# A four-layer graph network: the spread destination row loaded from ScalarE's queue, the third turn beside the first two, one TensorE wait out, node stores one round earlier

## What is computed

```python
x = _layernorm(x + _L0_gnn_ref(x, node_vec1, edge_attr_3, edge_attr_64, src, dst, ...), axis=-1)
x = _layernorm(x + _L1_gnn_ref(x, node_vec1, edge_attr_16, edge_attr_4, src, dst, ...), axis=-1)
x = _layernorm(x + _L2_gnn_ref(x, node_vec1, edge_attr_4, edge_attr_8, ..., src, dst, 16), axis=-1)
x = _layernorm(x + _L3_gnn_ref(x, node_vec1, src, dst, edge_attr_4, edge_attr_64, ...), axis=-1)
```

```python
amax = jax.lax.stop_gradient(jax.ops.segment_max(a, edge_dst, num_segments=n))
a = jnp.exp(a - amax[edge_dst])
a = a / (jax.ops.segment_sum(a, edge_dst, num_segments=n)[edge_dst] + 1e-12)
ns = jax.ops.segment_sum(vs * a[..., None], edge_dst, num_segments=n).reshape(n, H * H0)
```

```python
m_v3 = w5[:, :, None] * jnp.cross(ev, e1[:, None, :]) * _inv(2)
agg_s = jax.ops.segment_sum(mid_s, edge_dst, num_segments=n) * inv_nn
agg_v = jax.ops.segment_sum(mid_v, edge_dst, num_segments=n) * inv_nn
o_s = agg_s @ lin2_ws * a * _inv(S_MID)
...
pre_s = sc_s + o_s
pre_v = sc_v + o_v
scalars = jax.nn.silu(pre_s[:, :64])
gates = jax.nn.sigmoid(pre_s[:, 64:96])
gated = gates[:, :, None] * pre_v
```

## Time and profile before

| | us |
|---|---|
| median of 3 executions | 8838.66 |
| lowest, highest | 8814.75, 8842.85 |
| the profiled execution | 8821.47 |
| its span | 8819.7 |

### The profile page before, as it was taken

The page is one execution under the profiler, slowest core; times in us unless marked ns, Lnnn a source line. Parts: engine busy times, 40 slices in busy tenths (PEclk is TensorE's granted clock), DMA queues, the critical chain, the costliest instruction groups (busy, mean ns, idle before and its releaser), DMA issues. The chain is left out here.

```text
span 8819.7 us, 169625 instructions
## 1 busy us (share of the span) xinstructions
PE 6072.5 (69%) x36496; PEld 5115.7 (58%) x36496; DVE 6244.2 (71%) x20178; ACT 4194.7 (48%) x10003; POOL 4731.4 (54%) x4424
## 2 busy tenths in 40 slices
PE   3767777776657777777776666777666678884444
PEld 3555555555556666656665655666566567774443
DVE  6967777777658887866565775666688878785666
ACT  2544444443325555544444775444466645553333
POOL 3456666664445555545444554445466544445666
PEclk9977777776559999988888887889788899996666
DMA  6732222224753333334444665444466544443444
GB/s 185 242 119 75 75 76 75 77 71 133 205 168 105 108 110 103 106 92 120 116 117 131 198 196 158 116 116 120 122 178 179 172 120 129 128 122 115 128 128 124
DMA packets 774197, 1137.24 MB, mean 129 GB/s; under 512 B 322032, under 2 KB 410038, under 8 KB 773648
## 3 DMA queue, kind: packets, MB, share of 16 engines
q1 hardware_dynamic: 591952, 831.36, 30.2%
q0 software_dynamic: 182144, 304.74, 15.4%
HBM read 667.03 MB, written 472.87 MB: 129 GB/s over the span
## 5 line engine op out<-in xcount | busy, mean ns | idle before, releaser
L718 POOL DMA_INDIRECT agg<-seg_rows,node_idx x1568 | 1530.1, 976 | 1137.2 <-issue 924.4
L457 POOL DMA_INDIRECT erow<-e_rows,ids x1176 | 1220.0, 1037 | 1282.4 <-issue 1176.6
L397 PE MATMUL banks<-w_all,xt 128*128 128x128 f32 (+1 forms) x2352 | 559.7, 375 | 939.8 <-DVE stats L755 424.4
L397 PEld LDWEIGHTS banks<-w_all,xt 128*128 128x128 f32 x2352 | 439.2, 251 | 1027.9 <-issue 999.5
L767 POOL TENSOR_TENSOR stats<-stats,power 128x4 f32<-128x4 f32 (+1 forms) x392 | 524.8, 1339 | 544.6 <-DVE stats L755 341.9
L655 POOL DMA_INDIRECT row_of_dram<-where x392 | 431.7, 1101 | 559.0 <-DMA where<-place_dram 417.9
L487 PE MATMUL banks<-w_all,mid 128*128 128x128 f32 (+1 forms) x2744 | 457.9, 293 | 395.4 <-ACT hid_p L538 355.0
L400 PE MATMUL banks<-w_all,xt 128*128 128x128 f32 x3528 | 658.5, 339 | 0.0
L487 PEld LDWEIGHTS banks<-w_all,mid 128*128 128x128 f32 (+1 forms) x2744 | 327.7, 146 | 524.0 <-ACT hid_p L538 415.7
L400 PEld LDWEIGHTS banks<-w_all,xt 128*128 128x128 f32 x3528 | 620.9, 254 | 0.0
L544 ACT ACTIVATE radial<-banks 128x768 f32<-128x768 f32 (+1 forms) x294 | 248.6, 846 | 650.1 <-PE banks L497 362.1
(11 more groups left out here) (282 smaller groups left out, 18272.0 us busy)
## 6 DMA issues: line engine op xcount, KB each, us to landing
x_rows<-xo SPq DMA_DIRECT2D x294, 324.0 KB
xin<-x_rows SPq DMA_DIRECT2D x294, 324.0 KB
e_rows<-ets SPq DMA_DIRECT2D x294, 322.0 KB
dst_row<-in_dst_flat SPq DMA_DIRECT2D x294, 256.0 KB
xin<-in_x SPq DMA_DIRECT2D x196, 324.0 KB
seg_rows<-res SPq DMA_DIRECT2D x196, 322.0 KB
seg_rows<-res SPq DMA_DIRECT2D x98, 384.0 KB
seg_rows<-res SPq DMA_DIRECT2D x98, 338.0 KB
```

The source lines that it names most:

```text
L397: pe.matmul(flat[:, to + k * cols:to + (k + 1) * cols], of[:, k * P:(k + 1) * P], W(w_s), start=True, stop=True)
L457: pool.indirect_dma_start(erow[s.quad][:, t, 0:EROW], None, table, bass.IndirectOffsetOnAxis(ids[s.quad][:, t:t + 1], 0),).then_inc(edges_ ...
L718: pool.indirect_dma_start(agg[s.quad][:, t, 0:SUM_COLS[layer]], None, seg_rows[layer], bass.IndirectOffsetOnAxis(node_idx[s.slot][:, t, 0: ...
```

## The change

There are four edits.

- Edge softmax: `row_back` is no longer loaded by SP in `load` but by ScalarE, in a new function `load_row` at the head of ScalarE's list. It waits for the same count of `pre_step` as SP's `load` does and signals a semaphore of its own, which VectorE awaits before the comparison. ScalarE's other functions move from delays 0, 0, 2 to 3, 3, 5; what they wait for is unchanged.
- Edge stage of layer 3 (the lists of layers 1 and 2 come out as before): `turn_part` 2 on TensorE, and its copy on ScalarE, stand directly behind parts 0 and 1 instead of behind `weights`.
- Node stages 1 to 3: SP's stores stand one round earlier (5 and 6 instead of 6 and 7; in layer 3, 5 instead of 6). The title in a few words does not mention this.
- Node stage of layer 3: TensorE's wait for `sum_step` in `back` is left out. In layers 1 and 2 it stays.

```diff
-        soft_in = [signal(f"soft_in_{k}", 48, 2) for k in range(4)]
+        soft_in = [signal(f"soft_in_{k}", 32, 2) for k in range(4)]
+        row_back_in = [signal(f"row_back_in_{k}", 16, 2) for k in range(4)]
...
                     pipeline(pe, chunks, [
-                        (hidden, 0), (lambda s: turn_part(s, 0), 2), (lambda s: turn_part(s, 1), 2), (sums, 4), (weights, 0),
-                        *[(lambda s: turn_part(s, 2), 2)][:parts - 2], (linear, 2)])
+                        (hidden, 0), (lambda s: turn_part(s, 0), 2), (lambda s: turn_part(s, 1), 2),
+                        *[(lambda s: turn_part(s, 2), 2)][:parts - 2], (sums, 4), (weights, 0), (linear, 2)])
...
                     pipeline(act, chunks, [
-                        (hidden, 0), (lambda s: copy_part(s, 0), 2), (lambda s: copy_part(s, 1), 2), (weights, 0),
-                        *[(lambda s: copy_part(s, 2), 2)][:parts - 2], (sums, 4), *[(wrap, 0)][:crossed], (linear, 2)])
+                        (hidden, 0), (lambda s: copy_part(s, 0), 2), (lambda s: copy_part(s, 1), 2),
+                        *[(lambda s: copy_part(s, 2), 2)][:parts - 2], (weights, 0), (sums, 4), *[(wrap, 0)][:crossed], (linear, 2)])
...
-                        pipeline(sp, chunks, [loads, (lambda s: store_nodes(sp, s, x_rows[layer + 1]), 6),
-                                              (lambda s: store_e(sp, s, layer + 1), 7)])
+                        pipeline(sp, chunks, [loads, (lambda s: store_nodes(sp, s, x_rows[layer + 1]), 5),
+                                              (lambda s: store_e(sp, s, layer + 1), 6)])
                     else:
-                        pipeline(sp, chunks, [loads, (store_out, 6)])
+                        pipeline(sp, chunks, [loads, (store_out, 5)])
...
                         pe.wait_ge(xt_sb.sem, xt_sb.after(s.g + 1))
-                        pe.wait_ge(sum_step.sem, sum_step.after((s.g - 1 + with_e) * sum_steps - with_e * (sum_steps - read)))
+                        if with_e:
+                            pe.wait_ge(sum_step.sem, sum_step.after(s.g * sum_steps - (sum_steps - read)))
                         pe.wait_ge(pre_step.sem, pre_step.after((s.g - 1) * pre_steps))
...
-                        sp.dma_start(to_row[s.quad][:].rearrange("p t e -> p (t e)"),
-                                     inp["dst_flat"][0, bass.ds(c * CHUNK, CHUNK)].partition_broadcast(P)).then_inc(edges.sem, 16)
...
+                        dve.wait_ge(row_back_in[s.quad].sem, row_back_in[s.quad].after(s.quarter + 1))
                         dve.wait_ge(cols_in[b].sem, cols_in[b].after(s.quarter + 1))
...
-                    pipeline(act, chunks, [(exponentials, 0), (copy, 0), (sums, 2)])
+                    def load_row(s):
+                        c = chunks - 1 - s.g
+                        precompute(act, pre_step.after((s.g - 3) * 3))
+                        act.wait_ge(ready.sem, 1)
+                        act.wait_ge(pre_step.sem, pre_step.after((s.g - 3) * 3))
+                        act.dma_start(to_row[s.quad][:].rearrange("p t e -> p (t e)"),
+                                      inp["dst_flat"][0, bass.ds(c * CHUNK, CHUNK)].partition_broadcast(P)) \
+                            .then_inc(row_back_in[s.quad].sem, 16)
+
+                    pipeline(act, chunks, [(load_row, 0), (exponentials, 3), (copy, 3), (sums, 5)])
```

More of the change, by code:

```diff
@@ L1681, in edge_softmax @@
                 sig.passed(chunks // 2)
-            for sig, n in (*zip(soft_in, of_quad), *zip(soft_values, of_quad), *zip(cols_in, of_pair), *zip(place_in, of_pair), *zip(placed, of_pair)):
+            for sig, n in (*zip(soft_in, of_quad), *zip(row_back_in, of_quad), *zip(soft_values, of_quad), *zip(cols_in, of_pair), *zip(place_in, of_pair), *zip(placed, of_pair)):
                 sig.passed(n)
```

## The result

| | before, us | after, us |
|---|---|---|
| median of 3 executions | 8838.66 | 8614.98 |
| lowest, highest | 8814.75, 8842.85 | 8613.89, 8631.71 |
| the profiled execution, its span | 8821.47, 8819.7 | 8631.71, 8629.9 |

The account below looks back on a forecast made before the run. No engine is full; stages are bounded by waits between engines and, in softmax, SP's issuing. Gains 174 + 110 + 40 + 20 = 344 us, so 8838.66 - 344 = 8495 us, range 8425 to 8595 (0.8).

Parts of the forecast that it names:

- forecast 110: Edge stage of layer 3: the third turn placed earlier lets linear start earlier, saving 110 us (48 to 144).
- What is late next is VectorE: Edge stage of layer 3: VectorE's 1.48 us idle time limits the gain; rounds of 7.5 to 7.8 us expected.
- the turn's order brings nothing: Rival, edge stage of layer 3: VectorE or the gathers set the round, no 110 us gain, 8605 us; chance 0.09.
- forecast 20: Layer 1's node stage: stores issued a round sooner remove VectorE's wait for a store of xo, 20 us (0 to 32).
- up to some 3 us late costs nothing: Node stages: SP's new wait ahead of the next load is free, as that load is taken two rounds later.
- if SP's loads in layers 1 and 2 come late behind the stores: Node stages: a listed sign that the prediction is wrong, SP's loads delayed by the stores issued earlier.
- forecast 40: Softmax stage: moving the row's load to ScalarE frees SP's issuing time, saving 40 us (27 to 54).
- SP still never waiting: Softmax stage: a sign expected after the edit, with 4.3 us per chunk and a shorter wait for cols_back.
- the forecast's 0.45 per chunk: Softmax stage: SP's time freed by moving the row's load, 0.45 us per chunk, by 97 = 44 us.
- the transfers alone set the round: Rival, softmax stage: DMA transfers are the bound, so the 40 us is not gained, 8535 us; chance 0.05.
- forecast 174: Node stage of layer 3: without TensorE's wait, rounds fall from 8.49 to 6.7 us, set by GpSimd; 174 us (96 to 203).
- 344 forecast: Whole kernel: the sum of the four gains, 174 + 110 + 40 + 20 us, giving 8495 us.

Follow-up runs that it names:

- first measurement: The changed kernel with all four edits against the kernel before: 8614.98 against 8838.66 us, ratio 0.976.
- elsewhere: Later runs on other chips: single edits against the kernel before at 7871.93 us; the unedited changed kernel repeated, 7525.34 against 7872.55 us, ratio 0.9563.
- the run with a longer `linear`: The changed kernel with four matmuls of linear done twice in layer 3's edge stage: 7610.15 us, 85 more than the changed kernel.
- the kernel with the turn alone: The kernel before with only the third turned part moved ahead of the sums on TensorE and ScalarE: 7761.21 us, ratio 0.9859.
- The kernel with the stores alone: The kernel before with only the node stages' stores issued one round earlier: 7846.26 us, ratio 0.9964.
- the one with the row alone: The kernel before with only the softmax stage's spread row of destinations issued by ScalarE: 7839.66 us, ratio 0.9956.

## Why the prediction was wrong, step by step

**Edge stage of layer 3 (forecast 110, first measurement 16, elsewhere 105).** The step that failed is "What is late next is VectorE", with rounds of 7.5 to 7.8 us. It is TensorE that comes next. In the first measurement `linear`'s completion came late by 0.93 us in the median, and the median round was 8.54 us instead of 7.52. Where it came on time the mean round was 7.61 and the stage 105 us shorter. The sums (86 us of lateness and 22 us of lower clock, against 113.6 us of stage) and the run with a longer `linear` (0.8 us paid in full) show the path; what made TensorE late isn't known. That 110 came so near elsewhere is in part luck: TensorE's busy time per chunk (706.93 / 98 = 7.2 us) lies close to VectorE's (7.0), so the wrong bound stood at nearly the right place. My rival "the turn's order brings nothing" (8605) gave nearly the time, but for a reason that wasn't there: VectorE and the gathers set nothing.

It could have been read in the trace of before. Layer 1's edge stage, where `linear` follows without idle time, had ScalarE wait for something that no record showed running ("remote"); the kernel with the turn alone, in the same stage elsewhere, has no such wait:

```profile
ACT rows L562 <- remote: 93.0, 32, 3.9
ACT radial L544 <- remote: 73.4, 15, 9.9
```

```profile
ACT rows L562 <- PE banks L525: 44.8, 95, 2.2
```

That stage took 805.6 us in the first measurement and 558 elsewhere, of which TensorE's longer busy time can account for at most 612 - 527 = 85 us (clock 0.85 against 0.99). I read it only for its clock.

**Stores (forecast 20, first measurement -29, elsewhere 26).** The wait for `x_rows<-xo` went, as forecast. The step that failed in the first measurement is "up to some 3 us late costs nothing": it held where TensorE was on time, but where SP stood up to 8 us behind the stores the stage got longer. The prediction named this as a sign of being wrong ("if SP's loads in layers 1 and 2 come late behind the stores") and gave it neither a cost nor a chance.

**Softmax (forecast 40, stage 18 and 20).** The place was right, the size double. Elsewhere VectorE's wait for `cols_back` fell from 123.7 to 103.2 us, all that the stage gained; SP's three waits rose from 22.8 (17.6, 3.7, 1.5) to 45.1 us (33.3, 9.9, 1.9). So "SP still never waiting" failed. The time that SP does not spend waiting fell from 436.8 - 22.8 = 414.0 to 416.5 - 45.1 = 371.4 us: the 43 us freed are the forecast's 0.45 per chunk, but 22 of them went into SP's own waits and only 20 into the stage. The term that was mis-sized is the step from freed to gained, taken as one to one. `pen_back` on ScalarE shows the same more strongly: by the same reckoning it freed 52 us more (41.8 and then 81.0 us of SP's waits), of which 12 were gained. The rule of the Trainium skill that I weighed there (DMA: Bandwidth & Descriptors, Issuing engines are not separate DMA queues: the issuer changes only the sequencer's time) agrees with these numbers: time on SP's sequencer is all that the edit freed. That the transfers alone set the round is not shown either: with a quarter of the row the mean share of the DMA engines was 0.70 instead of 0.81, and the stage lost only 19 us.

```profile
SPq L1567 <- DVE aux L1625: 17.6, 26, 3.9
DVE matrix L1609 <- DMA cols_back<-in_dst_cols: 123.7, 48, 4.1
```

```profile
SPq L1568 <- DVE aux L1625: 33.3, 43, 5.5
DVE matrix L1609 <- DMA cols_back<-in_dst_cols: 103.2, 47, 4.4
```

(The kernel with the stores alone, then the one with the row alone.)

**Node stage of layer 3 (forecast 174, 167 and 170).** Right in place and size: GpSimd and the mix are late by turns, the rounds 6.77 us in the mean for 6.7. Two errors cancel in that: GpSimd's own work fell from 6.53 to about 6.1 us (8204.83 to 8209.74 + 1.16), and the idle time left ahead of it was 0.6 to 0.8 us instead of 0.2. TensorE has slack there, so its lateness cost nothing.

**The sum.** 344 forecast, 347 where TensorE was on time, 224 in the first measurement: 94 us of the difference of 120 are the turn, 49 the stores, 22 the softmax stage, 7 the node stage of layer 3, 172 in all. About 52 came back: 34 because the medians differ by 224 us and the profiled executions by 190 (8821.47 - 8631.71), and 18 in the other stages (the first node stage alone 21, 1237.2 to 1216.2, untouched).

## What to carry to other kernels

An edit that takes an engine's idle time out of a round is only worth what that engine really delivers. Ask also whether that engine, once dense, is the next bound itself. Ahead of such an edit, compare the end of its records with the start of what waits for them, in the stage of the same program that is already dense; a wait with no record behind it is the warning. Compare round by round with the start of the waiting instruction, as events can be missing from a trace. And of an issuing queue that is always busy, the time freed comes back only until its next wait: look up how long ago that wait's condition was met.

## What the runs showed of the hardware

The same program took 8838.66 us in one measurement and 7872 to 7876 us on three chips later (whether the first was one of them isn't known). Most of the difference lies in stages dense on TensorE: edge stage 1 805.6 against 558 us, edge stage 2 800 against 556, edge logits 1528 against 1245, while node stage 3 took 824 in both. In these three the granted clock was 0.75 to 0.88 instead of 0.85 to 0.99, and beyond that TensorE's completions came late against the modelled ends of its records, at a granted clock of 1.00 too: for `linear` in edge stage 1 by 134 us in 95 rounds, up to 5.2 us at once at that clock. TensorE's busy time doesn't show this part.

It was not TensorE alone. In layer 1's node stage of the kernel before, 94 of SyncE's 683 register, move and branch instructions took 0.3 to 0.7 us in the first measurement; in the same stage of the kernel with the turn alone, on the other chip, none took more than 0.1. So a cause that holds back several engines' instruction streams is a rival to one in TensorE, and no run here separates them.
